# Two of the four squares of a feed-forward block move from ScalarE to VectorE

## What is computed

```python
h = _layernorm(x) * (1 + ca) + sa
x = x + ga * attention(h)            # 16 heads of 8, rotary, causal softmax, projection
h = _layernorm(x) * (1 + cb) + sb
h = jnp.square(jax.nn.relu(jnp.einsum('bsd,fd->bsf', h, W_fc)))   # 128 -> 512 features
y = jnp.einsum('bsf,df->bsd', h, W_proj)                          # 512 -> 128
# y goes through 5 steps of a threshold (spike) model; x = x + gb * spikes / 5
```

## Time and profile before

| | |
|---|---|
| median of 3 runs | 451.45 us (449.46 to 453.56) |
| profiled execution | 447.9 us |
| its span, first to last instruction | 446.1 us |
| TensorE busy | 389.0 us, 87% |
| VectorE busy | 320.0 us, 72% |
| ScalarE busy | 263.3 us, 59% |
| GpSimd busy | 125.4 us, 28% |
| squares on ScalarE | 28, median 621 ns |

### The profile page before, as it was taken

The page is one execution under the profiler, slowest core; times in us unless marked ns, Lnnn a source line. Parts: engine busy times, 40 slices in busy tenths (PEclk is TensorE's granted clock), DMA queues, the critical chain, the costliest instruction groups (busy, mean ns, idle before and its releaser), DMA issues.

```text
span 446.1 us, 15629 instructions
## 1 busy us (share of the span) xinstructions
PE 389.0 (87%) x6603; PEld 251.9 (56%) x6603; DVE 320.0 (72%) x718; ACT 263.3 (59%) x459; POOL 125.4 (28%) x163
## 2 busy tenths in 40 slices
PE   3878989878999999998999989999999889888883
PEld 3326655545656665666557655666566646654653
DVE  6659987857884999478965998489956875631275
ACT  7203556576677666765686657766676558467522
POOL 7714211421341052403250244205340320040120
PEclk9989999999999999999999999999999999999999
DMA  6056463242424332232414241323224040011000
GB/s 212 24 159 168 110 203 107 67 128 70 113 60 114 77 101 79 92 95 49 137 62 133 54 135 60 110 62 96 79 82 106 25 137 17 16 38 28 3 24 25
DMA packets 26049, 38.53 MB, mean 86 GB/s; under 512 B 5796, under 2 KB 20716, under 8 KB 23692
## 3 DMA queue, kind: packets, MB, share of 16 engines
q1 hardware_dynamic: 25980, 37.53, 29.3%
HBM read 26.35 MB, written 8.65 MB: 78 GB/s over the span
## 4 chain that ended last, share of the span: by engine, by line
PE 42%; DVE 18%; DMA 12%; issue 9%; ACT 8%; SPq 6%; POOL 5%; ACTq 0%; POOLq 0%; DVEq 0%
PE o_bank L606 9%; PE d_bank L523 8%; PE t_bank L588 6%; DVE negmax L955 6%; PE s_bank L543 5%; DMA kf<-k_scr 3%; SPq L440 3%; ACT probs L809 3%; DVE xn L971 3%; PE a_bank L523 2%; DMA rden<-r_scr 2%; DMA r_scr<-rden_c 2%; DMA den<-o_raw 2%; PE t_bank L523 2%; SPq L444 2%
## 5 line engine op out<-in xcount | busy, mean ns | idle before, releaser
L955 DVE TENSOR_REDUCE negmax<-s_bank 128x1 f32<-128x512 f32 (+7 forms) x368 | 192.2, 565 | 66.3 <-PE s_bank L549 65.0
L809 ACT ACTIVATE probs<-t_bank 128x512 f32<-128x512 f32 x288 | 163.5, 595 | 87.5 <-PE t_bank L593 83.1
L543 PE MATMUL s_bank<-kf,qf 126*64 126x512 bf16 (+7 forms) x1024 | 118.5, 292 | 18.3 <-DVE negmax L955 15.4
L588 PE MATMUL t_bank<-qf,kf 128*64 128x512 bf16 (+7 forms) x1024 | 112.0, 288 | 10.2 <-ACT probs L809 8.9
L543 PEld LDWEIGHTS s_bank<-kf,qf 126*64 126x64 bf16 x1024 | 49.5, 109 | 50.4 <-DVE negmax L955 36.2
L606 PE MATMUL o_bank<-probs,v 128*32 128x512 f32 (+7 forms) x1024 | 75.2, 412 | 0.0
L549 PE MATMUL s_bank<-causal,identb 128*64 128x64 bf16 x1024 | 72.0, 194 | 0.0
L593 PE MATMUL t_bank<-causal_t,identb 128*64 128x64 bf16 x1024 | 64.4, 195 | 0.0
L588 PEld LDWEIGHTS t_bank<-qf,kf 128*64 128x64 bf16 x1024 | 41.2, 110 | 31.6 <-ACT probs L809 11.5
L593 PEld LDWEIGHTS t_bank<-causal_t,identb 128*64 128x64 bf16 x1024 | 47.6, 110 | 9.2
L549 PEld LDWEIGHTS s_bank<-causal,identb 128*64 128x64 bf16 x1024 | 46.6, 111 | 8.3 <-issue 8.2
(11 more groups left out here) (144 smaller groups left out, 441.6 us busy)
## 6 DMA issues: line engine op xcount, KB each, us to landing
qf<-q_scr SPq DMA_DIRECT2D x15, 576.0 KB
kf<-k_scr SPq DMA_DIRECT2D x45, 192.0 KB
q_scr<-parts SPq DMA_DIRECT2D x24, 128.0 KB, 1.7
k_scr<-parts SPq DMA_DIRECT2D x24, 128.0 KB, 1.7
xa<-in_x SPq DMA_DIRECT2D x8, 256.0 KB, 3.8
o_t<-o_raw SPq DMA_DIRECT2D x60, 32.0 KB, 2.2
rden<-r_scr SPq DMA_DIRECT2D x15, 128.0 KB
out_y<-count SPq DMA_DIRECT2D x7, 256.0 KB, 7.2
```

The source lines that it names most:

```text
L543: nc.tensor.matmul(bank[C * a:C * (a + 1), col:col + keys], qf[0:KS, slot, 2 * p + a, C * i:C * (i + 1)], kf[0:KS, slot, 2 * p + a, 0:keys ...
L588: nc.tensor.matmul(bank[C * a:C * (a + 1), col:col + w], kf[0:KX, slot, 2 * p + a, C * kb:C * (kb + 1)], qf[0:KX, slot, 2 * p + a, C * kb: ...
L809: nc.scalar.activation(probs[:, v, :], t_bank[u % 2][:, :], ACT.Exp, scale=SCALE).then_inc(e_done, 1)
L955: last = nc.vector.tensor_reduce(own[:, i, p:p + len(same)], cols, AX.X, ALU.max, negate=True)
```

## The change

VectorE gets a function `square` of its own, a multiplication of `relu` with itself, with the same two waits and the same count into `sq_done`. It makes blocks 1 and 2 (the second and third of the four), before the maxima of slots 32 and 34. ScalarE's table loses those two entries and keeps blocks 0 and 3. The last batch's tables are as they were. So 12 of 28 squares move, two in each of b = 1 to 6.

```diff
-            SQUARE_AT = {29: 0, 31: 1, 33: 2, 35: 3}
+
+            SQUARE_AT = {29: 0, 35: 3}
...
+            def square(b, i):
+                dve.wait_ge(d_free, freed(b, FC + i))
+                dve.wait_ge(d_ready, before(b, PROJ))
+                nc.vector.tensor_tensor(sq[:, i, :], relu[:, i, :], relu[:, i, :], ALU.mult).then_inc(sq_done, 1)
...
+            SQUARE_AT = {32: 1, 34: 2}
+
...
+                    if b < final and at in SQUARE_AT:
+                        square(b - 1, SQUARE_AT[at])
```

## The result

The changed kernel takes 447.96 us, median of 20 runs, against 449.92 us for the kernel before beside it: ratio 0.995, 95% interval 0.9928 to 0.9971. Every ratio in this text leaves out the runs that lie more than 1.5% above the fastest one of the same kernel, here three of the changed kernel and none of the kernel before; by the medians of all runs it would be 0.9957. Timed once more on another chip (12 runs, the first run under "Experiments") the ratio was 0.9989, interval 0.9959 to 1.0018. Weighted by their intervals the two give 0.9964, about 1.6 us less than before, with an interval from 0.9 to 2.4 us. The forecast was 0.8 us less, within 1%.

The account below looks back on a forecast made before the run. TensorE is busiest (87%), but the prediction read its pauses: only the third square pays, five batches by 0.16 us, 0.8 us off the median 451.45, forecast 450.6. Range 447.5 to 454.5.

Parts of the forecast that it names:

- The second square, cost and gain 0: Slot 31 of ScalarE to 32 of VectorE: ScalarE's freed time joins the pause before the cast; VectorE's idle time absorbs it.
- Who holds whom: Second square on VectorE beside GpSimd's sum: the sum begins 0.83 us earlier, so the square is held, about 1.0 us.
- this rival: GpSimd held: second square begins before GpSimd's sum, delaying the fourth product by up to 0.69 us a batch; 454.1, chance 0.12.
- The third square, cost 0: Slot 34 of VectorE: 0.69 us fits in the idle 2.04 us, with 0.4 us to spare for TensorE's bank.
- The third square, gain 0.16 us: Slot 33 of ScalarE: exponential 0.52 us sooner, but TensorE's pause before the t-bank matmul gives only 0.16 us a batch.
- The sixth batch, gain 0: Sixth batch, without rotary work, casts or such a TensorE pause: square fits VectorE's 0.96 us idleness; gain and cost 0.
- The advance is kept: VectorE's long unbroken run at 243.59 waits for TensorE, so it and the output transfers start earlier by the same amount.
- The time of 450.6 us: Whole kernel: forecast time, 0.8 us off the median of 451.45; chance of the forecast case 0.55.
- A batch repeats almost to the hundredth: Main loop: a batch takes about 48 us and repeats, so the one around 232 us was read for others.
- more is gained: Rival at the cast at 230.02: relu 0.52 us sooner, the 0.90 us pause shrinks; 3.4 us gained, 448.0, chance 0.13.
- The small form of the first: GpSimd's sum starts slower by 0.13 us a batch, eating the gain; 451.3, chance 0.15 together with the nothing-moves case.
- Nothing moves: Rival at the t-bank pause: the 0.16 us is not gained or is given back at a transfer; 451.45, chance 0.15.

Follow-up runs that it names:

- the first run under "Experiments": The changed kernel with no edit, timed again on another chip against the kernel before; ratio 0.9989 (0.9959 to 1.0018).

## Why the prediction was right, and which term was mis-sized

- **The second square, cost and gain 0: right.** Alone it moved no stretch (13.18 us) and no time (1.0018). The freed time of ScalarE went into the pause before the cast, 0.57 to 1.08 us; I had said about 1.1. On VectorE it took 1.07 us, against "about 1.0", and the next maximum began with no idle time.
- **Who holds whom: right.** GpSimd's sum stayed at 1.27 us with the square in slot 32. In slot 30 it was 1.72 us and the fourth product 0.45 us later. I had priced this rival at up to 0.69 us; it is 0.45.
- **The third square, cost 0: right.** 0.69 us in an idle time; with a reciprocal of 1.75 us behind it 0.49 us a batch appear on TensorE. The room beyond the idle time, which I had put at 0.4 us, is 0.37.
- **The third square, gain 0.16 us: right in mechanism, half the size.** The step that failed is "TensorE, however, is not free before 235.13 - 0.16 = 234.97". By the chain ScalarE had 0.52 us to give, and TensorE was indeed next, but it could begin at 234.80: the t-bank's matmul starts 0.03 us after the start of the one ahead of it when nothing holds it, not after its end. The gain is 0.33 us, five times, 1.7 us instead of 0.8. The pause of 0.90 us was likewise worth 1.07 when it went away.
- **The sixth batch, gain 0: right.** 11.88 us before and after.
- **"The advance is kept": held, within what can be seen.** 1.7 us locally; 0.5 to 2.2 us by the two timings.
- **The time of 450.6 us: 2.6 us too high, and inside the range partly by luck.** The kernel before had 451.45 us over its first 3 runs and 449.92 over 20, so 1.5 us of the difference are the base from which I subtracted. Another 0.9 us are what the third square gained beyond the sum, and the rest is spread. 447.96 is only 0.5 us from the lower end of the range.
- **"A batch repeats almost to the hundredth": wrong as it stands.** From bank to bank the batches of the kernel before take 47.9 to 49.1 us. What repeats to the hundredth is the stretch that I read, and the sum needed only that.
- **The rival "more is gained"** named 3.4 us through the 0.90 us pause. The pause stayed at 0.89 to 0.90 us in all five batches, so it did not happen. The first median, 447.96 us, equals this rival's 448.0 by coincidence: the rival's figure starts from the 451.45 that was too high.
- **The other rivals.** The small form of the first (GpSimd's sum slower by 0.13 us) did not come, as the sum kept its 1.27 us. "Nothing moves" is out by the second pause, which is gone in all five batches.

## What to carry to other kernels

Giving work from one engine to another pays only what the waiting engine could have used: read the pause behind each moved instruction, not the instruction's length, and count a pause of TensorE from start to start, against a place where the same two matmuls follow without one. When an instruction is moved, follow every transfer that waits for it and what stands behind that transfer on the issuing queue; here that took back 0.94 of 1.07 us. Where an engine waits at two places for the same kind of transfer, count both before one of them is moved. And when a timing and a profile disagree by more than the change, cut the profile into stretches that repeat and stretches that don't, before a story is made of either.

## What was not expected of the hardware

- A VectorE multiplication with both inputs in SBUF and a GpSimd instruction went one after the other: the square behind GpSimd's running instruction, and GpSimd's next instruction behind the waiting square, with 0.54 to 0.55 us for VectorE after its release (0.69 us undisturbed). The Trainium skill says this of the read port they share (SBUF — State Buffer, "Who interferes with whom"); these runs agree. It also says that the loser is blocked for the whole of the other's instruction; GpSimd lost 0.45 us to a square that ran on for 0.55 us, and the 0.1 us between are not explained, and neither is why the square needs 0.14 us less after its release than by itself.
- Twenty runs of the changed kernel spread over 8 us (443.36 to 451.32), five times the change, and of the twelve on another chip one took 465.66 us at a mean granted clock of 0.854 (0.979 to 0.992 in the others). One run of the kernel with the maxima's transfer first and all squares on ScalarE took 742.15 us. Neither of the two has a profile, and their causes are open. TensorE's stretches without a transfer in them repeat to 0.03 us from batch to batch in the profiles of the kernel before and of the changed one.
